# The last pair of batches attends one batch after the other, and four steps of its first batch run on GpSimd

## The chip, the cores and the metric

The kernel runs on one core of one Trainium2 chip. The metric is device time in microseconds (us), from the program's start to its end. TensorE (PE in the profile; PEld is its weight load) multiplies, VectorE (DVE), ScalarE (ACT) and GpSimd (POOL) do elementwise work, and SyncE (SP) issues the transfers.

## The reference

A layer with two parts over x of 32 batches, 512 tokens, 256 features, all float32:

```python
x = x + attention(layernorm(x))    # logits = phi phi^T * decay / temp, causal, softmax, times V
x = x + slots(layernorm(x))        # below

h = gelu(concat(x, slot_mean) @ w1.T + b1)
top = top_k((h @ w2.T + b2) / (abs(tau) + 0.1), 8)
alpha = softmax over the 8 chosen of 64 slots, zero elsewhere    # (T, 64)
gi = (alpha.T @ x) / (alpha.sum(0) + 1e-8)                        # (64, 256)
S_new = GRU(gi, slots)
out = (alpha @ (S_new @ wv.T + bv)) @ wo.T + bo
```

phi has 64 features per token; it comes from a tanh charge, random Fourier features and a combining matrix.

## The kernel before, in words

The batches go in 16 pairs. Pair k holds batches 2k (d = 0) and 2k + 1 (d = 1); the last pair is k = 15, batches 30 and 31. Every engine has its own queue, in which the steps of several pairs are mixed in an order written out by hand: a loop for the steady part and a long list for the end. An engine runs its queue strictly in that order; a step waits on semaphores that others raise, and all behind it wait with it.

The steps of a pair, each a function called with (k, ...), and the engine of each:

- **Attention.** phi (PE) and qk_full (DVE) give QK, in which batch d of the pair lies in partitions 64d to 64d + 63. The 512 query rows of a batch are four blocks of 128 rows; block i sees (i + 1) x 128 columns. logits(k, j) (PE) does blocks 0 and 1 (j = 0), block 2 (j = 1) or block 3 (j = 2), in each for the two batches alternately, into two banks of a ring L. Then for each of the eight row blocks n of a pair: row_max (DVE), expo (ACT), e_t (PE, i + 1 transpositions), probs_t (ACT, makes Eh), probs_low (DVE, makes El), values (PE, 3(i + 1) matmuls, the last i + 1 of which read El), attended (DVE, adds to X), lm_stats (DVE). Before, block n of every pair is row block n // 2 of batch n % 2, so the two batches go alternately.
- **Second norm.** lm_scale (six small operations of lm_variance_ops, and a power, on POOL), lm_norm (four operations, POOL) make xm; xm_t (PE), xm_copy (ACT), xm_low (DVE).
- **Routing.** hidden (PE), gelu (ACT), route (PE), rt_out (ACT), rt_t (PE), top (DVE, two max and two replace each, for half a batch), shift (DVE), shift8 (POOL), route_exp (ACT), weight_sum and chosen (DVE), alpha (POOL).
- **Slots.** gather (PE), gathered (DVE), gi_t (PE), gi_copy (ACT), gx_rz and gx_n (PE), gates, candidate (DVE), tanh (ACT), slot_change (POOL), new_slots (DVE), slot_v (PE), slot_values (DVE), al_t (PE), al_copy (ACT).
- **Output.** out_mm (PE), finish (DVE), store (SP).

In the last pair, before, the second norm (but for its power), shift8 and alpha of both batches run on DVE (end_scale, end_norm, end_shift, end_alpha, a for batch 30 and b for batch 31), and routing is done batch by batch (end_route, end_rt_t; gather(15) does batch 30's four matmuls, then batch 31's). warm(12) is twelve matmuls whose result nobody reads. residual adds X through an identity matmul, full array, two of 512 columns.

Lines that the rows name: L321 transpositions, L415 logits, L443 values, L497 end_route, L506 end_rt_t, L531 gather, L546 gates of the GRU, L656 residual; L1103 probs_low, L1119 attended, L1130 lm_stats, L1158 max of top; L246 and L258 the first and the last operation of lm_variance_ops, L1572 the power, L268 lm_norm, L287 alpha.

## Time and profile before

| | us |
|---|---|
| median of 3 runs | 689.96 (689.7 to 691.14) |
| the profiled execution | 689.95 |
| its span, first to last instruction | 688.1 |
| TensorE busy | 672.6 (98%) |
| VectorE busy | 605.0 (88%) |
| ScalarE busy | 514.3 (75%) |
| GpSimd busy | 386.9 (56%) |

Busy time is the time in which an engine had an instruction under way; matmuls overlap, and their ends are modelled, so their starts are the surer reading. The granted clock of TensorE is at its full level over the span but for the first slice and the last microseconds.

### The profile page before, as it was taken

The page shows a single profiled execution, that of the slowest core. Times are in us where ns is not written, and L with a number is a line of the kernel's source. Part 1 is how long each engine was busy: PE and PEld are TensorE (multiplying, and loading weights), DVE is VectorE, ACT ScalarE, POOL GpSimd, SP SyncE. Part 2 cuts the span into 40 slices and gives each one's busy share as a digit, 9 for nine tenths or more (in the row PEclk, how much of TensorE's full clock was granted, in tenths as well). Part 3 has the DMA queues.
Part 4 walks back from the last instruction along what each step waited for, and adds up shares of the span by engine and source line. Part 5 has one row for each costly group of instructions (what it writes and reads, how often), then busy time and mean ns, then how long its engine had stood idle before and what let it go on. Part 6 is the DMA issues. An engine that isn't in the chain of part 4 may idle for free.

```text
span 688.1 us, 15845 instructions
## 1 busy us (share of the span) xinstructions
PE 672.6 (98%) x4626; PEld 541.6 (79%) x4626; DVE 605.0 (88%) x2001; ACT 514.3 (75%) x1478; POOL 386.9 (56%) x818
## 2 busy tenths in 40 slices
PE   8999999999899999999999999999999999999996
PEld 5867878787697887879798787979878787978774
DVE  6688998797989898998989899898989989899984
ACT  4979889777596896959698695968879596875461
POOL 3727867362665747376565737556583756655200
PEclk9999999999999999999999999999999999999999
DMA  8343020204233050323215042421504242121004
GB/s 237 109 153 93 1 63 1 63 2 137 49 103 81 20 158 11 122 63 118 67 38 148 2 125 61 123 63 57 130 1 134 53 123 62 63 62 63 1 32 152
DMA packets 49115, 54.11 MB, mean 79 GB/s; under 512 B 6212, under 2 KB 40582, under 8 KB 49030
## 3 DMA queue, kind: packets, MB, share of 16 engines
q1 hardware_dynamic: 48260, 52.57, 27.7%
q8 instruction: 38, 0.62, 0.4%
q10 hardware_dynamic: 770, 0.53, 0.3%
q14 instruction: 47, 0.39, 0.2%
HBM read 20.58 MB, written 16.78 MB: 54 GB/s over the span
## 4 chain that ended last, share of the span: by engine, by line
PE 87%; SPq 3%; DVE 3%; ACT 2%; issue 2%; POOL 2%; DMA 1%; DVEq 0%; ACTq 0%; POOLq 0%
PE ps L321 17%; PE ps L349 16%; PE ps L443 15%; PE ps L476 6%; PE ps L546 6%; PE ps L415 6%; PE ps L531 4%; PE ps L641 4%; PE ps L488 2%; SPq L1717 2%; PE ps L392 2%; PE ps L617 2%; PE ps L398 2%; PE ps L395 2%; PE ps L308 1%
## 5 line engine op out<-in xcount | busy, mean ns | idle before, releaser
L241 POOL TENSOR_TENSOR Z<-Z,QB 128x512 f32<-128x512 f32 x60 | 77.4, 1290 | 80.6 <-ACT Z L834 78.8
L779 ACT ACTIVATE xn<-X,rs 128x255 f32<-128x255 f32 x128 | 66.4, 599 | 72.0 <-POOL rs L1563 72.0
L349 PE MATMUL ps<-W1h,xh 128*128 128x354 f32 x256 | 88.6, 346 | 0.0
L443 PE MATMUL ps<-Vh,Eh 128*128 128x256 f32 x320 | 88.6, 304 | 0.0
L349 PE MATMUL ps<-W1h,xl 128*128 128x354 f32 x256 | 83.2, 325 | 0.6 <-DVE xl L1039 0.5
L349 PE MATMUL ps<-W1l,xh 128*128 128x354 f32 x256 | 83.0, 324 | 0.0
L443 PE MATMUL ps<-Vl,Eh 128*128 128x256 f32 x320 | 80.9, 280 | 0.0
L845 ACT ACTIVATE E<-ps,nmax 128x128 f32<-128x128 f32 (+3 forms) x128 | 67.9, 536 | 9.7 <-DVE nmax L1095 9.5
L1103 DVE TENSOR_TENSOR El<-ps,Eh 128x128 fp32r<-128x128 f32 (+3 forms) x128 | 61.7, 483 | 13.2 <-ACT Eh L855 11.7
L1046 DVE TENSOR_TENSOR Vl<-ps,Vh 128x256 fp32r<-128x256 f32 x128 | 53.5, 419 | 21.7 <-ACT Vh L804 19.3
L268 POOL TENSOR_SCALAR xm<-X,rs 128x256 f32<-128x256 f32 x120 | 68.0, 581 | 2.2 <-POOL rs L1572 1.0
L855 ACT ACTIVATE Eh<-ps 128x128 fp32r<-128x128 f32 (+3 forms) x128 | 55.6, 445 | 11.8 <-PE ps L321 10.2
L443 PEld LDWEIGHTS ps<-Vh,Eh 128*128 128x128 f32 x320 | 60.3, 188 | 4.8 <-DVE X L1119 2.4
L1095 DVE CUSTOM_DVE_ANT_0 ps<-ps,causal 128x128 f32<-128x128 f32 (+3 forms) x128 | 60.9, 499 | 2.8 <-PE ps L415 2.8
L1119 DVE SCALAR_TENSOR_TENSOR X<-ps,rinv,X 128x256 f32<-128x256 f32 x128 | 59.5, 474 | 1.6 <-PE ps L443 1.2
L443 PEld LDWEIGHTS ps<-Vl,Eh 128*128 128x128 f32 x320 | 60.4, 189 | 0.2
L443 PE MATMUL ps<-Vh,El 128*128 128x256 f32 x320 | 58.7, 281 | 1.3 <-DVE El L1103 1.3
L321 PE MATMUL ps<-ident,E 128*128 128x128 f32 x320 | 55.3, 277 | 0.7 <-DVE El L1103 0.4
L1130 DVE BATCH_NORM_STATS2 stats<-X 128x6 f32<-128x256 f32 x128 | 51.8, 416 | 0.1
L804 ACT ACTIVATE Vh<-ps 128x256 fp32r<-128x256 f32 x128 | 51.7, 404 | 0.0
L349 PEld LDWEIGHTS ps<-W1h,xh 128*128 128x128 f32 x256 | 48.4, 189 | 2.9 <-issue 1.1
L321 PEld LDWEIGHTS ps<-ident,E 128*128 128x128 f32 x320 | 36.7, 140 | 17.5 <-issue 10.5
(245 smaller groups left out, 1961.9 us busy)
## 6 DMA issues: line engine op xcount, KB each, us to landing
X<-in_x SPq DMA_DIRECT2D x32, 512.0 KB, 4.4
xmT<-Z SPq DMA_DIRECT2D x120, 128.0 KB, 2.3
out_x<-X SPq DMA_DIRECT2D x30, 512.0 KB, 3.7
out_x<-X SPq DMA_DIRECT2D x4, 256.0 KB, 2.5
X<-in_gru_whhT SPq DMA_DIRECT2D x1, 768.0 KB
wih<-in_gru_wihT SPq DMA_DIRECT2D x1, 768.0 KB, 6.1
X<-in_W_v ACTq DMA_DIRECT2D x1, 256.0 KB, 4.5
X<-in_W_outT ACTq DMA_DIRECT2D x1, 256.0 KB
```

The lines of the kernel that those rows point to most:

```text
L241: e.tensor_tensor(Z[:, i + 1, :], Z[:, i, :], QB[:, :], ALU.mult).then_inc(s["zm"], 1)
L268: ins = e.tensor_scalar(xm[:, b % 3, t, 0:D], X[:, b % NX, t, :], rs2[:, d, 2, t:t + 1], rs2[:, d, 1, t:t + 1], ALU.add, ALU.mult)
L321: ins = e.transpose(p[0:m, j * 128:j * 128 + 128], block_in, ident[:, :])
L349: ins = e.matmul(p[:, 0:FEATS], x[:, d, c, t * 128:t * 128 + 128], w[:, c, :], start=j == 0, stop=j == 5)
L443: ins = e.matmul(p[:, 0:D], w[:, r % 2, j * 128:j * 128 + 128], v[:, (2 * k + d) % 4, j, :], start=z == 0, stop=z == len(parts) - 1)
L779: ins = e.activation(xn[:, d, t, 0:D - 1], X[:, b % NX, t, 0:D - 1], ACT.Identity, bias=rs[:, d, 2, t:t + 1], scale=rs[:, d, 1, t:t + 1])
L845: e.activation(E[:, r % 3, 0:w], at["lg", r], ACT.Exp, bias=nmax[:, r % 8:r % 8 + 1], scale=-1.0, accum_out=rsum[:, r % 8:r % 8 + 1]).then ...
L855: e.activation(Eh[:, r % 2, 0:w], at["E", r][:, 0:w], ACT.Copy).then_inc(s["eh"], 1)
L1046: e.tensor_tensor(Vl[:, b % 4, t, :], at["vs", b, t][:, 0:D], Vh[:, b % 4, t, :].bitcast(FP), ALU.subtract).then_inc(s["vl"], 1)
L1095: e.tensor_tensor_reduce(at["lg", r], at["lg", r], causal[:, N - w:N], 1.0, 3e38, ALU.add, ALU.min, nmax[:, r % 8:r % 8 + 1]).then_inc(s[" ...
L1103: e.tensor_tensor(El[:, r % 2, 0:w], at["E", r][:, 0:w], Eh[:, r % 2, 0:w].bitcast(FP), ALU.subtract).then_inc(s["ET"], 1)
L1119: e.scalar_tensor_tensor(X[:, b % NX, i, :], at["av", r][:, 0:D], rinv[:, r % 8:r % 8 + 1], X[:, b % NX, i, :], ALU.mult, ALU.add).then_in ...
```

## The change

Three things are done together.

1. In the last pair, block n is row block n % 4 of batch n // 4, so batch 30's four blocks come first and batch 31's four after them. A new end_logits(d, j) makes the logits of one batch; the waits are renumbered (place, width, shared, rows_done).
2. Batch 30's variance chain, normalization, shift8 and alpha go back from VectorE to GpSimd. Batch 31's stay on VectorE.
3. The order of the end, from the last pair's first norm on, is new on TensorE, ScalarE, VectorE and GpSimd. Some instances: rt_t(14) comes behind values(15, 4) and e_t(15, 6), where it came behind values(15, 3) and e_t(15, 4); top(14) comes behind lm_stats(15, 3), attended(15, 4) and probs_low(15, 5) on VectorE; finish(13, 1, 0) comes behind the last alpha. From gather(15) on TensorE's order is as before. SyncE's order is not changed.

```diff
--- before.py
+++ after.py
@@ -242,7 +242,7 @@
 
         def lm_variance_ops(e, k, d):
             b = 2 * k + d
-            e.wait_ge(s["lm_s"], 8 * k + 7 + d)
+            e.wait_ge(s["lm_s"], rows_done(k, d))
...
@@ -293,6 +293,20 @@
+        def place(k, n):
+            return divmod(n, 4) if k == NP - 1 else (n % 2, n // 2)
+
+        def width(k, n):
+            return place(k, n)[1] * 128 + 128
+
+        def shared(k, n):
+            if k == NP - 1:
+                return 1 if n % 4 == 0 else 0
+            return 2 if n < 2 else 0
+
+        def rows_done(k, d):
+            return 8 * k + 4 * d + 4 if k == NP - 1 else 8 * k + d + 7
...
@@ -415,6 +429,19 @@
+            def end_logits(d, j):
+                k = NP - 1
+                p, before = L.take(s["E"], 8 * k + 4 * d + j + 2)
+                if d == j == 0:
+                    e.wait_ge(s["qk"], 2 * k + 2)
+                if before:
+                    e.wait_ge(*before)
+                for i, c in ((0, 0), (1, 128)) if j == 0 else ((j + 1, 0),):
+                    rows, w = slice(i * 128, i * 128 + 128), i * 128 + 128
+                    at["lg", 8 * k + 4 * d + i] = p[:, c:c + w]
+                    e.matmul(p[:, c:c + w], QK[own(d), 0, rows], QK[own(d), 1, 0:w], start=True,
+                             stop=True, skip_group_check=True).then_inc(s["lg_mm"], 1)
...
-                transposes(p, [E[:, r % 3, j * 128:j * 128 + 128] for j in range(n // 2 + 1)]).then_inc(s["ET_t"], 1)
+                transposes(p, [E[:, r % 3, j * 128:j * 128 + 128] for j in range(place(k, n)[1] + 1)]).then_inc(s["ET_t"], 1)
...
-                i, d = divmod(n, 2)
+                d, i = place(k, n)
...
-                if n == 0:
-                    e.wait_ge(s["vl"], 8 * k + 8)
+                if i == 0 and (n == 0 or k == NP - 1):
+                    e.wait_ge(s["vl"], 8 * k + (4 * d + 4 if k == NP - 1 else 8))
...
-            e_t(14, 6); values(14, 5); values(14, 6); e_t(14, 7); phi(15); gather(13); logits(15, 0)
-            out_mm(12, 0); gi_t(13); values(14, 7); e_t(15, 0); xm_t(14, 0, 0); e_t(15, 1); gx_rz(13)
-            values(15, 0); e_t(15, 2); xm_t(14, 0, 1); gx_n(13); out_mm(12, 1); logits(15, 1); e_t(15, 3)
-            values(15, 1); xm_t(14, 1, 0); hidden(14, 0); xm_t(14, 1, 1); values(15, 2); hidden(14, 1)
-            e_t(15, 4); logits(15, 2); route(14); values(15, 3); rt_t(14); e_t(15, 5); slot_v(13)
-            values(15, 4); e_t(15, 6); values(15, 5); e_t(15, 7); al_t(13); values(15, 6); values(15, 7)
-            gather(14); out_mm(13, 0); gi_t(14); gx_rz(14); xm_t(15, 0, 0); xm_t(15, 0, 1); xm_t(15, 1, 0)
-            gx_n(14); xm_t(15, 1, 1); hidden(15, 0); hidden(15, 1); end_route(0); al_t(14); end_rt_t(0)
-            end_route(1); out_mm(13, 1); end_rt_t(1); slot_v(14); warm(12); gather(15); out_mm(14, 0)
...
+            e_t(14, 6); slot_v(12); values(14, 6); phi(15); gather(13); end_logits(0, 0); end_logits(0, 1)
+            e_t(14, 7); gi_t(13); out_mm(12, 0); end_logits(0, 2); e_t(15, 0); values(14, 7); e_t(15, 1)
+            gx_rz(13); end_logits(1, 0); end_logits(1, 1); xm_t(14, 0, 0); values(15, 0); xm_t(14, 0, 1)
+            values(15, 1); e_t(15, 2); gx_n(13); e_t(15, 3); e_t(15, 4); hidden(14, 0); end_logits(1, 2)
+            out_mm(12, 1); xm_t(14, 1, 0); xm_t(14, 1, 1); values(15, 2); hidden(14, 1); values(15, 3)
+            route(14); e_t(15, 5); values(15, 4); e_t(15, 6); rt_t(14); values(15, 5); slot_v(13); al_t(13)
+            values(15, 6); e_t(15, 7); xm_t(15, 0, 0); values(15, 7); gather(14); out_mm(13, 0); gi_t(14)
+            xm_t(15, 0, 1); gx_rz(14); xm_t(15, 1, 0); xm_t(15, 1, 1); hidden(15, 0); gx_n(14); hidden(15, 1)
+            end_route(0); al_t(14); end_route(1); end_rt_t(0); slot_v(14); end_rt_t(1); out_mm(13, 1)
+            warm(12); gather(15); out_mm(14, 0); gi_t(15); al_t(15); end_gx_r(); end_gx_nz(); out_mm(14, 1)
...
-                w = (n // 2 + 1) * 128
-                e.wait_ge(s["nmax"], r + 3 if n < 2 else r + 1)
+                w = width(k, n)
+                e.wait_ge(s["nmax"], r + 1 + shared(k, n))
...
+            gelu(14, 1); probs_t(15, 4); rt_out(14); probs_t(15, 5); probs_t(15, 6); expo(15, 7)
+            route_exp(14, 0); probs_t(15, 7); route_exp(14, 1); al_copy(13); xm_copy(15, 0, 0); gi_copy(14)
...
-                b, i = 2 * k + n % 2, n // 2
+                d, i = place(k, n)
+                b = 2 * k + d
                 e.wait_ge(s["av_mm"], r + 1)
-                e.wait_ge(s["rinv"], 4 * k + i + 1)
+                e.wait_ge(s["rinv"], 4 * k + n // 2 + 1)
...
-            def end_scale_a_setup():
-                e.wait_ge(s["lm_n"], B - 2)
-                lm_variance_ops(e, NP - 1, 0)
-
             def end_scale_b_setup():
+                e.wait_ge(s["lm_v"], B - 1)
                 lm_variance_ops(e, NP - 1, 1)
 
-            def end_norm_a_setup():
-                e.wait_ge(s["lm_n"], B - 2)
-                lm_norm_ops(e, NP - 1, 0)
-
             def end_norm_b_setup():
+                e.wait_ge(s["lm_n"], B - 1)
                 lm_norm_ops(e, NP - 1, 1)
 
-            def end_shift_a_setup():
-                e.wait_ge(s["dm8"], B - 2)
-                shift8_ops(e, NP - 1, 0)
-
             def end_shift_b_setup():
+                e.wait_ge(s["dm8"], B - 1)
                 shift8_ops(e, NP - 1, 1)
 
-            def end_alpha_a_setup():
-                e.wait_ge(s["am"], B - 2)
-                alpha_ops(e, NP - 1, 0)
-
             def end_alpha_b_setup():
+                e.wait_ge(s["am"], B - 1)
                 alpha_ops(e, NP - 1, 1)
...
-            attended(15, 3); top(14, 0, 0); top(14, 0, 1); top(14, 1, 0); shift(14, 0); top(14, 1, 1)
-            attended(15, 4); probs_low(15, 5); shift(14, 1); slot_values(13); probs_low(15, 6)
-            lm_stats(15, 3); attended(15, 5); chosen(14, 0); inverse(15, 3); weight_sum(14, 0)
-            probs_low(15, 7); weight_sum(14, 1); chosen(14, 1); attended(15, 6); lm_stats(15, 4)
-            lm_stats(15, 5); lm_stats(15, 6); attended(15, 7); end_scale_a_setup(); gathered(14)
-            lm_stats(15, 7); end_scale_b_setup(); finish(13, 0, 0); end_norm_a_setup(); end_norm_b_setup()
...
+            attended(15, 3); lm_stats(15, 3); attended(15, 4); probs_low(15, 5); top(14, 0, 0); top(14, 0, 1)
+            probs_low(15, 6); top(14, 1, 0); weight_sum(14, 0); shift(14, 0); top(14, 1, 1); shift(14, 1)
+            chosen(14, 0); attended(15, 5); weight_sum(14, 1); probs_low(15, 7); chosen(14, 1)
+            slot_values(13); lm_stats(15, 4); inverse(15, 3); lm_stats(15, 5); attended(15, 6)
+            attended(15, 7); lm_stats(15, 6); lm_stats(15, 7); gathered(14); end_scale_b_setup()
+            xm_low(15, 0, 0); finish(13, 0, 0); end_norm_b_setup(); xm_low(15, 0, 1); gates(14)
+            finish(13, 0, 1); xm_low(15, 1, 0); xm_low(15, 1, 1); candidate(14); new_slots(14); top(15, 0, 0)
+            top(15, 0, 1); top(15, 1, 0); shift(15, 0); top(15, 1, 1); weight_sum(15, 0); chosen(15, 0)
+            shift(15, 1); end_shift_b_setup(); slot_values(14); weight_sum(15, 1); chosen(15, 1)
+            end_alpha_b_setup(); finish(13, 1, 0); finish(13, 1, 1); gathered(15); finish(14, 0, 0)
...
@@ -1566,14 +1580,14 @@
-                if k < NP - 1:
+                if k < NP - 1 or d == 0:
...
             @live
             def lm_norm(k, d):
-                if k == NP - 1:
+                if k == NP - 1 and d:
...
-            rnorm(15); slot_change(12); phase(15); power(15, 0); power(15, 1); power(15, 2); shift8(13, 0)
+            slot_change(12); rnorm(15); phase(15); power(15, 0); power(15, 1); power(15, 2); shift8(13, 0)
             power(15, 3); shift8(13, 1); alpha(13, 0); alpha(13, 1); lm_scale(14, 0); lm_norm(14, 0)
-            lm_scale(14, 1); lm_norm(14, 1); slot_change(13); shift8(14, 0); shift8(14, 1); alpha(14, 0)
-            alpha(14, 1); lm_scale(15, 0); lm_scale(15, 1); slot_change(14)
+            lm_scale(14, 1); lm_norm(14, 1); slot_change(13); lm_scale(15, 0); shift8(14, 0); lm_norm(15, 0)
+            shift8(14, 1); alpha(14, 0); alpha(14, 1); lm_scale(15, 1); slot_change(14); shift8(15, 0)
+            alpha(15, 0)
```

## Rows read from the trace of the kernel before

**Rows 1.** The page: engines' busy time, then VectorE groups with count, busy us, mean ns.

```profile
PE 672.6 (98%) x4626; PEld 541.6 (79%) x4626; DVE 605.0 (88%) x2001; ACT 514.3 (75%) x1478; POOL 386.9 (56%) x818
...
L1103 DVE TENSOR_TENSOR El<-ps,Eh 128x128 fp32r<-128x128 f32 (+3 forms) x128 | 61.7, 483 | 13.2 <-ACT Eh L855 11.7
...
L1119 DVE SCALAR_TENSOR_TENSOR X<-ps,rinv,X 128x256 f32<-128x256 f32 x128 | 59.5, 474 | 1.6 <-PE ps L443 1.2
L1130 DVE BATCH_NORM_STATS2 stats<-X 128x6 f32<-128x256 f32 x128 | 51.8, 416 | 0.1
```

**Rows 2.** Busy time by stretch: length, each engine's busy us (instructions), clock, DMA.

```profile
639.71:649.28 9.57, 9.01 (x73) 8.19 (x73) 9.50 (x46) 4.85 (x13) 1.71 (x4) 1.00 0.01 2
643.13:669.08 25.95, 23.95 (x166) 18.69 (x165) 22.85 (x92) 12.54 (x24) 3.98 (x5) 1.00 0.07 22
```

**Rows 3.** The chain that ended last, from 616 on: start us, us, what.

```profile
619.32 1.74 PE ps L531 x16
...
621.06 0.86 PE ps L415 x8
...
630.04 0.65 PE ps L415 x4
...
636.09 1.06 PE ps L415 x4
...
644.31 0.87 PE ps L321 x8
645.18 2.81 PE ps L443 x24
647.99 2.29 PE ps L531 x16
...
660.59 1.05 PE ps L497 x2
...
665.17 0.24 PE ps L506 x4
...
669.15 2.81 PE ps L531 x16
...
677.98 1.91 PE ps L656 x4
```

**Rows 4.** TensorE in order of time: start us, us, in brackets idle before and releaser.

```profile
639.04 0.63 PE L321 MATMUL ps<-ident,hT 128*128 128x128 f32 x4
...
643.69 0.62 PE L443 MATMUL ps<-Vh,El 128*128 128x256 f32 x3 [0.56 <-DVE El L1103]
...
652.30 2.02 PE L546 MATMUL ps<-GI,wih 128*128 128x128 f32 x16 [0.56 <-ACT GI L903]
...
662.49 0.43 PE L506 MATMUL ps<-ident,hT 64*128 64x64 f32 x4 [0.28 <-ACT hT L886]
```

**Rows 5.** VectorE in order of time, from top(14) to the last alpha.

```profile
639.71 0.36 DVE L1158 MAX8 m<-ps 128x8 f32<-128x64 f32 x2
...
648.81 0.47 DVE L1119 SCALAR_TENSOR_TENSOR X<-ps,rinv,X 128x256 f32<-128x256 f32 x1
...
649.98 0.16 DVE L258 TENSOR_TENSOR rs<-rs 128x4 f32<-128x4 f32 x1
...
652.34 0.16 DVE L258 TENSOR_TENSOR rs<-rs 128x4 f32<-128x4 f32 x1
...
653.03 2.66 DVE L268 TENSOR_SCALAR xm<-X,rs 128x256 f32<-128x256 f32 x8
...
669.44 0.43 DVE L287 TENSOR_TENSOR AL<-lg,asum 128x256 f32<-128x256 f32 x1
```

**Rows 6.** GpSimd in order of time: the second norm of batch 28.

```profile
619.28 0.20 POOL L246 TENSOR_TENSOR mv<-stats 128x8 f32<-128x8 f32 x1 [0.23 <-DVE stats L1130]
...
621.01 1.04 POOL L1572 TENSOR_TENSOR rs<-rs,half 128x4 f32<-128x4 f32 x1
...
622.22 2.18 POOL L268 TENSOR_SCALAR xm<-X,rs 128x256 f32<-128x256 f32 x4 [0.17 <-POOL rs L1572]
```

More of the change, by code:

```diff
@@ L742, in _ @@
                 e_t(n, 7); values(n, 6); values(n, 7); phi(p); gather(f); logits(p, 0); out_mm(m, 0); gi_t(f)
-            xn_t(15, 0, 0); xn_t(15, 0, 1); gx_rz(12); proj(15, 0, 0); gx_n(12); e_t(14, 0); xn_t(15, 1, 0)
-            proj(15, 0, 1); xn_t(15, 1, 1); proj(15, 0, 2); proj(15, 0, 3); e_t(14, 1); logits(14, 1)
-            out_mm(11, 1); xm_t(13, 0, 0); proj(15, 1, 0); values(14, 0); xm_t(13, 0, 1); e_t(14, 2)
-            proj(15, 1, 1); proj(15, 1, 2); proj(15, 1, 3); values(14, 1); e_t(14, 3); xm_t(13, 1, 0)
@@ L747, in _ @@
-            xm_t(13, 1, 1); hidden(13, 0); q_t(15); hidden(13, 1); values(14, 2); e_t(14, 4); values(14, 3)
-            route(13); logits(14, 2); z_t(15); e_t(14, 5); rt_t(13); values(14, 4); al_t(12); slot_v(12)
-            e_t(14, 6); values(14, 5); values(14, 6); e_t(14, 7); phi(15); gather(13); logits(15, 0)
-            out_mm(12, 0); gi_t(13); values(14, 7); e_t(15, 0); xm_t(14, 0, 0); e_t(15, 1); gx_rz(13)
-            values(15, 0); e_t(15, 2); xm_t(14, 0, 1); gx_n(13); out_mm(12, 1); logits(15, 1); e_t(15, 3)
@@ L757, in _ @@
-            end_route(1); out_mm(13, 1); end_rt_t(1); slot_v(14); warm(12); gather(15); out_mm(14, 0)
-            gi_t(15); al_t(15); end_gx_r(); end_gx_nz(); out_mm(14, 1); residual(); slot_v(15); out_mm(15, 0)
-            out_mm(15, 1)
+            xn_t(15, 0, 0); xn_t(15, 0, 1); gx_rz(12); proj(15, 0, 0); proj(15, 0, 1); e_t(14, 0); gx_n(12)
+            xn_t(15, 1, 0); xn_t(15, 1, 1); proj(15, 0, 2); proj(15, 0, 3); logits(14, 1); out_mm(11, 1)
+            xm_t(13, 0, 0); proj(15, 1, 0); xm_t(13, 0, 1); values(14, 0); e_t(14, 1); proj(15, 1, 1)
@@ new lines, in _ @@
+            proj(15, 1, 2); values(14, 1); e_t(14, 2); e_t(14, 3); proj(15, 1, 3); xm_t(13, 1, 0)
+            xm_t(13, 1, 1); hidden(13, 0); e_t(14, 4); values(14, 2); hidden(13, 1); values(14, 3); q_t(15)
+            logits(14, 2); route(13); z_t(15); e_t(14, 5); rt_t(13); values(14, 4); values(14, 5); al_t(12)
+            e_t(14, 6); slot_v(12); values(14, 6); phi(15); gather(13); end_logits(0, 0); end_logits(0, 1)
+            e_t(14, 7); gi_t(13); out_mm(12, 0); end_logits(0, 2); e_t(15, 0); values(14, 7); e_t(15, 1)
@@ L1520, in _ @@
-            mirror(15); quarter_turn(15); attended(14, 3); lm_stats(14, 2); probs_low(14, 4); inverse(14, 2)
-            lm_stats(14, 3); row_max(14, 6); row_max(14, 7); top(13, 0, 0); top(13, 0, 1); attended(14, 4)
-            probs_low(14, 5); top(13, 1, 0); top(13, 1, 1); shift(13, 0); probs_low(14, 6); shift(13, 1)
-            slot_values(12); chosen(13, 0); attended(14, 5); inverse(14, 3); weight_sum(13, 0); chosen(13, 1)
-            lm_stats(14, 4); lm_stats(14, 5); weight_sum(13, 1); attended(14, 6); lm_stats(14, 6); qk_full(15)
@@ L1541, in _ @@
[L1541 to L1545 removed]
+            slot_values(11); ln_stats(15, 0, 0); weight_sum(12, 1); chosen(12, 1); ln_stats(15, 0, 1)
@@ new lines, in _ @@
+            attended(13, 6); lm_stats(13, 3); ln_stats(15, 1, 0); attended(13, 7); qk_full(14)
+            ln_stats(15, 1, 1); lm_stats(13, 4); gathered(12); row_max(14, 0); finish(11, 0, 0)
+            finish(11, 0, 1); row_max(14, 1); xn_low(15, 0, 0); xn_low(15, 0, 1); lm_stats(13, 5); gates(12)
+            row_max(14, 2); lm_stats(13, 6); row_max(14, 3); v_low(15, 0, 0); inverse(14, 0); probs_low(14, 0)
+            lm_stats(13, 7); v_low(15, 0, 1); candidate(12); inverse(14, 1); v_low(15, 0, 2); xn_low(15, 1, 0)
@@ new lines, in _ @@
+            lm_stats(14, 0); lm_stats(14, 1); row_max(14, 6); row_max(14, 7); lm_stats(14, 2)
+            probs_low(14, 5); top(13, 0, 0); attended(14, 4); lm_stats(14, 3); top(13, 0, 1); attended(14, 5)
+            shift(13, 0); top(13, 1, 0); probs_low(14, 6); top(13, 1, 1); chosen(13, 0); shift(13, 1)
+            lm_stats(14, 4); weight_sum(13, 0); chosen(13, 1); weight_sum(13, 1); inverse(14, 3)
+            slot_values(12); qk_full(15); attended(14, 6); gathered(13); row_max(15, 0); row_max(15, 1)
@@ L1609, in shift8 @@
             def shift8(k, d):
-                if k == NP - 1:
+                if k == NP - 1 and d:
                     return
@@ L1616, in alpha @@
             def alpha(k, d):
-                if k == NP - 1:
+                if k == NP - 1 and d:
                     return
```

79 lines of the change are left out of this document (33 added, 46 removed).

## The prediction

> **What bounds the kernel now.** I read the page first: TensorE is busy 98% of the span, VectorE 88% [rows 1]. So whatever the change does, it must act through the 2% in which TensorE stands, or through the length of TensorE's own work. Then the busy time by stretch: between 643.13 and 669.08 TensorE is busy 23.95 of 25.95 us, so 2.0 us of idle lie there, and between 639.71 and 649.28 it is VectorE that is full, 9.50 of 9.57 us [rows 2]. Then the chain of waits, for the pitch of each group of matmuls: the reader is to see there that some groups, of equal size, take different times [rows 3]. Then the order of time of TensorE, for its waits: 0.56 us for El of row block 5 of the last pair, 0.56 us for GI, 0.28 us for the routing logits [rows 4]. Last, VectorE's and GpSimd's own sequences, for the chain that the last batch goes through after its last values [rows 5, 6]. The tail from gather(15) on has the same order on TensorE before and after, so I carry it over unchanged; what I need is how much later or earlier gather(15) ends.
>
> **Pairs of logits are split: +1.8 us of TensorE.** logits(15, j) issues the two batches' matmuls alternately; they have a contraction of 64 and lie in the two halves of the partitions. Its three calls take 0.86, 0.65 and 1.06 us, 2.57 us for 2560 streamed columns [rows 3]. end_logits issues one batch at a time. What a 512-column matmul costs when its neighbour does not use the other half: end_route, one matmul, takes 1.05 us, as much as the 1.06 us of a pair of such; residual's two full-array ones take 1.91 us together [rows 3]. At residual's 0.96 us per 512 columns, 2560 columns take 4.8 us: +2.2 us; at end_route's, 5.25 us: +2.7. The lower end comes from gather: with the batches alternating it takes 1.74 us, in gather(15), where one batch follows the other, 2.81 us, a factor of 1.61 [rows 3], so +1.6 us. That factor is under 2 because the second batch's run begins while the first's is under way; in the new order this can happen once, where out_mm(12, 1) stands behind end_logits(1, 2), and I take 0.4 us off for it (one of its four matmuls). Value taken: 2.2 - 0.4 = +1.8 us, nearer to residual, since most neighbours of the new blocks are full-array matmuls. Nothing below zero: the same columns are streamed.
>
> The rows show two 64-deep matmuls of one size running in the time of one. The Trainium skill says the same of such matmuls in "TensorE: Matmul & The Clock Gate", section "Part 3: Packing small matmuls — row/col tiling", and adds that matmuls start and end strictly in program order. By that rule nothing would be gained at out_mm(12, 1), and the sum of this part would be +2.2; by gather(15)'s row it is +1.8.
>
> **The routing chain of pair 14 starts later.** rt_t(14) started at 639.04 [rows 4], and top(14) on VectorE at 639.71 [rows 5]. In the new order TensorE has done more of pair 15 when it comes to rt_t(14): values 0 to 4 with blocks of 1, 2, 3, 4, 1 (33 matmuls) where there were values 0 to 3 with 1, 1, 2, 2 (18): 15 x 0.117 (2.81 / 24) = 1.8 us; transposes of E 16 where there were 9: 7 x 0.109 (0.87 / 8) = 0.8 us [rows 3]; and the 1.8 us of the logits. Together 4.3 us (1.76 + 0.76 + 1.8); everything else that stood ahead of it still does. So top(14) begins at about 639.71 + 4.3 = 644.0. I assume that TensorE meets no new wait up to there; ScalarE and VectorE have more room in that part than later.
>
> **VectorE from there to attended(15, 7).** Before: 639.71 to 648.81 + 0.47 = 649.28, 9.57 us without a gap [rows 2, 5]. Now attended(15, 4), probs_low(15, 5) and lm_stats(15, 3) stand ahead of top(14), and lm_stats(15, 6) behind attended(15, 7): 0.47 + 0.48 + 0.42 + 0.42 = 1.8 us fewer [rows 1]. 644.0 + 7.8 = 651.8, which is 2.5 us later than before. This part is full on VectorE, so what it loses on TensorE the 0.56 us wait for El [rows 4] gives back only in part: TensorE stands at gather(14) for alpha(14, 1) as before, where gather took 2.29 us for work of 1.74 [rows 3].
>
> **The last batch's norm.** Before, the first of the two variance chains ended at 649.98 + 0.16 = 650.14 and the second at 652.50 [rows 5], 3.22 us behind attended(15, 7). The first chain, 0.86 us of it, is now on GpSimd, lm_stats(15, 6), 0.42 us, comes in: 2.8 us, so 654.6. GpSimd's power, about 1.1 us with its hand-over [rows 6], is hidden behind nothing as before. Then only four normalizations stand in VectorE's queue where there were eight in 2.66 us [rows 5]: 1.33 us. xm of batch 31 is ready at 654.6 + 1.2 + 1.33 = 657.1; it was ready at 653.03 + 2.66 = 655.69. So of 2.5 us that are late, 1.1 is given back here by the work that went to GpSimd, and +1.4 us stay. TensorE would be there earlier, at about 656, since it has only gather, out_mm, gi_t, one transposition and gx_rz in between, so it waits about 1 us.
>
> **From there to gather(15).** Before, 655.69 to 669.15, 13.46 us [rows 3, 5]. The set of TensorE's work is the same, xm_t(15, 1, 0) to warm, but end_rt_t(0) now stands behind end_route(1), so its wait of 0.28 us and the start-up behind it (its four 64-column transpositions take 0.24 us elsewhere) go [rows 3, 4]: -0.45, 13.0 us. gather(15) starts at 670.1, +0.95 us. VectorE is in step with that: alpha of batch 31 ended at 669.44 + 0.43 = 669.87, 4.7 us behind end_rt_t(1) at 665.17 [rows 3, 5]; end_rt_t(1) stays 4.0 us ahead of gather(15) (out_mm has taken slot_v's place behind it, both of one size), so alpha comes at 670.8, and gather(15)'s second half, which needs it, is as much later, +0.95. The two finish(13, 1) behind it fit under gather(15)'s 2.81 us, and the stores that they release have some 8 us until the next one: free.
>
> **The four steps on GpSimd** cost there 1.7 us (variance chain, 619.28 to 621.01), 1.0 (power) and 2.2 (normalization) [rows 6] besides shift8 and alpha, with nobody waiting for them as long as they are done before xm_t(15, 0, 0) and hidden(15, 0): values(15, 3) ends 1.95 us before rt_t(14) (route, as long as a pair of logits, 1.05, values(15, 4), three matmuls, 0.35, and five transpositions, 0.55), at 641.4; attended and lm_stats make it 642.3, so lm_norm(15, 0) ends near 642.3 + 1.8 + 1.1 + 2.2 = 647.4, or 647.7 with shift8(14, 0) ahead of it. In its queue behind it stand shift8(14, 1), alpha(14, 0) and alpha(14, 1). VectorE has m8 of (14, 1) at about 647.5: a tie, priced at nothing here and below as a rival.
>
> **Sum.** The profiled execution took 689.95 us, the median of the runs is 689.96, so both are one number here. 689.95 + 0.95 = 690.9 us, +0.14%. A measurement of this kernel can tell about 0.2% (1.4 us) from no change: 688.6 to 691.3 is no change.
>
> **Rivals.** *Faster: the waits go and the halves cost little.* All idle of 643.13 to 669.08, 2.0 us, and the 0.55 us of gather(14) are gained because VectorE has 10 instructions for statistics and 4 normalizations fewer, and the logits cost nothing: 689.95 - 2.55 = 687.4. With the logits at their lower end, +1.6, even this gives only 689.0. It decides if top(14) begins before about 641.5 at the new place. For it: VectorE is the engine without a gap there [rows 2]. Against it: rows 3 for the halves.
> *Neutral: the logits cost nothing, the rest as worked out:* everything above follows top(14) one for one, 690.9 - 1.8 = 689.1.
> *Slower: GpSimd's queue becomes the bound.* If batch 30's statistics come late, lm_norm(15, 0), 2.2 us in one piece, holds shift8(14, 1); ScalarE's exp waits for it, then weight_sum(14, 1) on VectorE, and behind that in the same queue probs_low(15, 7), for which values(15, 7) waits. There are some 0.7 us of work between (shift, chosen, attended) before it bites; from lm_norm ending at 648.4 on, each us costs a us. With 1 us late and the logits at their upper end: 690.9 + 1.0 + 0.9 = 692.8. For it: the order puts a 2.2 us step ahead of a 0.3 us one that others need. Likewise probs_t(15, 7) stands on ScalarE behind an exp that waits for shift(14, 0), which I priced at nothing.
>
> **Chances.** Forecast 0.45 (0.35 of it within 0.2%, 0.10 above, its upper part being only 0.4 us from the border); neutral 0.15; faster 0.20; slower by GpSimd 0.20. So faster 0.20, same 0.50, slower 0.30. The forecast's own range is 690.0 to 691.8; with the cases on both sides 688.2 to 692.9.
>
> **What the changed profile would show.** Groups of the new logits line whose 512-column matmul takes about 1 us alone; rt_t(14) near 643.4 and the first max of top(14) near 644.0; no wait of TensorE for El of block 5, but one of about 1 us before xm_t(15, 1, 0) released by VectorE's normalization; lm_norm of batch 30 on GpSimd between 645 and 648 and nobody waiting for what stands behind it; gather(15) starting near 670.1 and the same 16 us from its end to the end of the span. The prediction is wrong if the logits of one batch take as little as the pair did, if a wait arises earlier than 640 (the middle of the order is new too, and I walked only its end), or if weight_sum(14, 1) waits for GpSimd.

## The result, and the profile after

The changed kernel takes **692.38 us** (median of 8 runs, 691.47 to 694.4); the kernel before, on the same chip, 689.83 us (median of 8 runs, 689.01 to 691.14). The ratio is 1.0037, with an interval of 1.0024 to 1.005: slower by 2.55 us, or 0.37%. The forecast was 690.9 us with a range of 688.2 to 692.9. The time lies in the range, but above what the forecast's own case allowed (691.8), and on the slower side, to which 0.3 was given. It is in the range only because that takes in the slower rival's time, and that rival's mechanism did not occur; the hit is in part luck.

The profiled execution has a span of 690.9 us, where the one before had 688.1: +2.8 us. The page, first the engines' busy time, then VectorE's groups (count, busy us, mean ns, idle before them):

```profile
PE 675.4 (98%) x4626; PEld 542.6 (79%) x4626; DVE 602.9 (87%) x1989; ACT 514.9 (75%) x1478; POOL 389.1 (56%) x830
...
L1130 DVE TENSOR_TENSOR El<-ps,Eh 128x128 fp32r<-128x128 f32 (+3 forms) x128 | 61.8, 484 | 13.4 <-ACT Eh L882 12.1
...
L1147 DVE SCALAR_TENSOR_TENSOR X<-ps,rinv,X 128x256 f32<-128x256 f32 x128 | 59.6, 474 | 2.3 <-PE ps L470 1.9
```

Against [rows 1] twelve instructions have gone from VectorE to GpSimd (VectorE 2.1 us less, GpSimd 2.2 us more), and TensorE has as many instructions as before but is busy 2.8 us longer. The durations of single instructions are those of before. So the change of the span is there in TensorE's busy time, and the question is where.

TensorE in order of time, gather(12) (of batches 24 and 25) and gather(15) (of the last pair); first the kernel before, then the changed one (start, duration):

```profile
580.71 1.91 PE L531 MATMUL ps<-xm,AL 128*64 128x257 f32 x16
...
669.08 2.88 PE L531 MATMUL ps<-xm,AL 128*64 128x257 f32 x16
```

```profile
580.66 1.91 PE L558 MATMUL ps<-xm,AL 128*64 128x257 f32 x16
...
671.63 3.13 PE L558 MATMUL ps<-xm,AL 128*64 128x257 f32 x16
```

At gather(12) the two profiles agree within 0.05 us, and up to the end of gather(15) the changed one loses 2.80 us: (671.63 + 3.13) - (669.08 + 2.88). Nothing is lost or won after it: 16.1 us remain in both. The profiled executions of the experiments differ at gather(12) by up to 4 us (experiment 2, which changes the loop, apart), so below everything is counted from there.

The chain that ended last, in the changed kernel (start, us, what):

```profile
615.17 3.26 DMA xmT<-Z
...
618.48 1.08 PE ps L412 x4
619.56 1.74 PE ps L558 x16
621.30 1.49 PE ps L442 x6
...
623.60 1.06 PE ps L668 x8
624.66 0.85 PE ps L442 x2
...
629.18 1.49 PE ps L442 x6
...
635.93 0.42 PE ps L442
636.35 0.22 PE ps L668
636.56 0.22 PE ps L442
636.78 1.07 PE ps L668 x5
...
649.79 0.41 DVE X L1147
...
650.24 1.67 PE ps L470 x12
...
671.70 3.06 PE ps L558 x16
```

L442 is the new line of the logits. Its rows give 1.49 + 0.85 + 1.49 + 0.42 + 0.22 = 4.47 us where [rows 3] have 2.57 us. At the top of the fence the chain runs through a transfer: the last third of phi(15) waits for it, which it did not in the kernel before.

TensorE in order of time, its waits in brackets (rt_t(14) without one):

```profile
644.62 0.61 PE L335 MATMUL ps<-ident,hT 128*128 128x128 f32 x4
...
649.51 0.66 PE L335 MATMUL ps<-ident,xm 128*128 128x128 f32 x4 [0.78 <-DVE lg L1198]
...
658.74 1.06 PE L335 MATMUL ps<-ident,xm 128*128 128x128 f32 x8 [0.53 <-DVE xm L268]
```

All the waits of [rows 4], for El, GI and the routing logits, are gone. rt_t(14) starts 5.58 us later than before. The 0.78 us stand ahead of xm_t(15, 0, 0), which needs batch 30's normalization. The page names a subtraction on VectorE (L1198) as releaser, but the instruction reads xm, and xm's last write, on GpSimd, ended at 647.06 + 2.16 = 649.22 (below): that is very likely the wait. The prediction had nobody waiting for this step. The wait cost next to nothing all the same: in the chain above values(15, 7), which stands behind xm_t(15, 0, 0), starts at 650.24 and is put down to attended(15, 5) on VectorE (649.79 + 0.41).

Busy time from top(14) to the end of attended(15, 7) (length, then PE, PEld, VectorE, ScalarE, GpSimd):

```profile
645.28:653.24 7.96, 7.11 (x55) 6.16 (x55) 7.89 (x43) 4.63 (x11) 5.21 (x11) 1.00 0.01 2
```

This stretch answers to the first of [rows 2]: VectorE is full again (7.89 of 7.96 us), but in 7.96 us, not 9.57. VectorE itself, in order of time:

```profile
645.28 0.36 DVE L1186 MAX8 m<-ps 128x8 f32<-128x64 f32 x2
...
652.37 0.86 DVE L1147 SCALAR_TENSOR_TENSOR X<-ps,rinv,X 128x256 f32<-128x256 f32 x2
...
657.21 1.38 DVE L268 TENSOR_SCALAR xm<-X,rs 128x256 f32<-128x256 f32 x4
...
670.23 0.42 DVE L1198 TENSOR_TENSOR lg<-ps,m 128x256 f32<-128x256 f32 x1
670.56 0.55 DVE L277 TENSOR_TENSOR m8s<-m 128x32 f32<-128x32 f32 x1
...
672.33 0.42 DVE L287 TENSOR_TENSOR AL<-lg,asum 128x256 f32<-128x256 f32 x1 [0.19 <-DVE lg L1214]
```

attended(15, 7) ends at 653.23 (649.28 before), xm of batch 31 is ready at 657.21 + 1.38 = 658.59 (655.69 before), and alpha of batch 31 at 672.75 (669.87 before). So the loss is 5.6 us at top(14), 3.95 at attended(15, 7), 2.90 at xm, 2.55 at the start of gather(15) and 2.80 at its end. GpSimd, in the same stretch:

```profile
645.82 1.04 POOL L1586 TENSOR_TENSOR rs<-rs,half 128x4 f32<-128x4 f32 x1
646.83 0.24 POOL L277 TENSOR_TENSOR m8s<-m 128x32 f32<-128x32 f32 x1
647.06 2.16 POOL L268 TENSOR_SCALAR xm<-X,rs 128x256 f32<-128x256 f32 x4
649.19 0.24 POOL L277 TENSOR_TENSOR m8s<-m 128x32 f32<-128x32 f32 x1
```

shift8(14, 1), the fourth row, starts right behind the normalization of 2.16 us, and also right behind the last step of top(14, 1) on VectorE, which ended at 649.12: the tie on which the slower rival hung came out even, and VectorE did not stand ahead of weight_sum(14, 1).

### The profile page after: what moved, and what is told of

The parts are those of the page before. It is cut to its first block, busy times and chain, and to the rows that moved or that the text cites. A ratio compares the mean times of both kernels' runs of the same rounds, so it can differ in the third digit from the quotient of the medians.

```text
span 690.9 us, 15845 instructions
## 1 busy us (share of the span) xinstructions
PE 675.4 (98%) x4626; PEld 542.6 (79%) x4626; DVE 602.9 (87%) x1989; ACT 514.9 (75%) x1478; POOL 389.1 (56%) x830
## 4 chain that ended last, share of the span: by engine, by line
PE 85%; SPq 3%; DVE 3%; ACT 3%; POOL 2%; issue 2%; DMA 2%; DVEq 0%; POOLq 0%; ACTq 0%
PE ps L335 17%; PE ps L363 16%; PE ps L470 14%; PE ps L573 6%; PE ps L503 6%; PE ps L429 5%; PE ps L558 4%; PE ps L668 4%; SPq L1732 2%; PE ps L515 2%; PE ps L412 2%; PE ps L406 2%; PE ps L644 2%; PE ps L409 2%; POOL Z L241 1%
## 5 line engine op out<-in xcount | busy, mean ns | idle before, releaser
L268 POOL TENSOR_SCALAR xm<-X,rs 128x256 f32<-128x256 f32 x124 | 69.8, 576 | 2.2 <-POOL rs L1586 1.0
L1169 DVE TENSOR_TENSOR xmL<-ps,xmT 128x512 fp32r<-128x512 f32 x62 | 42.2, 686 | 9.9 <-ACT xmT L893 9.6
```

Source lines behind the costliest of these rows:

```text
L268: ins = e.tensor_scalar(xm[:, b % 3, t, 0:D], X[:, b % NX, t, :], rs2[:, d, 2, t:t + 1], rs2[:, d, 1, t:t + 1], ALU.add, ALU.mult)
```

## The experiments

The table first. Its time columns are medians (the ratio with its interval is against the kernel before, run beside each); the other columns are worked out from TensorE's order of time in each profile: the start of gather(13), (14), (15) behind the start of gather(12), how long gather(15) took, and where it ended.

| kernel | median us (runs) | ratio to before | g(13) | g(14) | g(15) | took | end | end against before |
|---|---|---|---|---|---|---|---|---|
| before | 689.83 (8) | | 38.44 | 67.21 | 88.37 | 2.88 | 91.25 | |
| changed | 692.38 (8) | 1.0037 (1.0024 to 1.005) | 38.73 | 71.18 | 90.97 | 3.13 | 94.10 | +2.85 |
| before, logits split | 693.72 (6) | 1.0054 (1.0036 to 1.0072) | 38.51 | 70.62 | 91.79 | 2.88 | 94.67 | +3.42 |
| changed, e_t first | 693.12 (6) | 1.005 (1.0033 to 1.0067) | 39.50 | 71.52 | 91.31 | 3.12 | 94.43 | +3.18 |
| changed, end_rt_t first | 693.23 (6) | 1.0045 (1.0031 to 1.006) | 38.26 | 70.82 | 90.92 | 3.12 | 94.04 | +2.79 |
| before, four steps on GpSimd | 690.91 (11) | 1.0017 (1.0008 to 1.0026) | 38.43 | 67.18 | 89.33 | 2.88 | 92.21 | +0.96 |
| changed, four steps on VectorE | 697.46 (4) | 1.0112 (1.0098 to 1.0125) | 38.25 | 75.88 | 95.36 | 3.16 | 98.52 | +7.27 |
| the same, better placed | 694.49 (5) | 1.0063 (1.0051 to 1.0076) | 38.42 | 72.65 | 92.47 | 3.16 | 95.63 | +4.38 |
| changed, shift8 first | 692.15 (6) | 1.0033 (1.0021 to 1.0045) | 38.27 | 70.80 | 90.61 | 2.88 | 93.49 | +2.24 |
| changed, logits twice | 696.66 (4) | 1.0101 (1.0085 to 1.0116) | 38.51 | 75.30 | 95.09 | 3.12 | 98.21 | +6.96 |
| before, end_route(1) first | 690.74 (11) | 1.0011 (1.0001 to 1.002) | 38.47 | 67.23 | 89.18 | 3.00 | 92.18 | +0.93 |

The last column and the medians agree within about half a microsecond, so this column can be used where a median is too coarse, though each row of it is one execution. For the experiments the kernel before had medians of 689.94, 689.65 and 689.9 us. The changed kernel's own row contains a wait of 0.4 to 0.5 us ahead of gather(13) that most of the other executions go without (experiment 4), so an experiment that goes without it looks up to that much better beside this row than it is; where it matters the count starts at gather(13).

**1. The split of the logits alone.**

```
-  phi(15); gather(13); logits(15, 0); out_mm(12, 0); gi_t(13); values(14, 7)
+  phi(15); gather(13); out_mm(12, 0); logits_of_one(15, 0, 0); gi_t(13); logits_of_one(15, 0, 1); values(14, 7)
...
-  logits(15, 1); e_t(15, 3)
+  logits_of_one(15, 1, 0); e_t(15, 3); logits_of_one(15, 1, 1)
-  e_t(15, 4); logits(15, 2); route(14)
+  logits_of_one(15, 2, 0); e_t(15, 4); logits_of_one(15, 2, 1); route(14)
```

> The kernel before, with one thing of the change: in the last pair, the two batches' logits are issued apart, with a full-array step between them; the order of attention, the engines of all steps and the rest of the order stay. Theory (half of the change's loss is TensorE's own work, because a 64-deep matmul without a partner in the other half takes as long as a pair): the changed kernel's logits took 4.69 us where the pairs took 2.57, so TensorE gets 2.1 us more; at most 0.56 us of it vanish in the wait for El at 643.69, so 1.5 to 2.1 us slower than before, and the 512-column blocks take about 1 us each in the chain. Rival (the logits lie under VectorE's work, and the loss comes from the order): within 0.3 us of before.

Measured: +3.8 us by the medians, +3.42 us by the profile. The chain of this kernel, at the new line (L430) and at two neighbours (L656 out_mm, L458 values):

```profile
624.11 1.06 PE ps L656 x8
625.17 0.65 PE ps L430 x4
...
626.18 0.85 PE ps L430 x4
627.03 1.60 PE ps L458 x12
...
634.20 0.64 PE ps L430 x2
...
635.20 0.84 PE ps L430 x2
...
640.95 1.05 PE ps L430 x2
...
642.48 1.05 PE ps L430 x2
```

The six rows of L430 make 5.08 us against 2.57 us for the same matmuls in pairs: +2.51 us. Most of the remaining 0.9 us stands in the rows of neighbours, each against the same group in the chain of before: out_mm(12, 0) 1.06 for 0.86, values(14, 7) 1.60 for 1.41, values(15, 1) 0.56 for 0.36, e_t(15, 4) 0.48 for 0.33: 0.74 us for four groups that now begin anew. The result is above what was expected. It is also more than the whole change costs, though it splits more finely than the change does (5.08 against 4.47 us for the logits): the rest of the change does give something back.

**2. The same split in ten pairs of the loop.** Three edits of the same kind in the loop's own order, where the calls also change places with neighbours.

> The kernel before, with the same separation of the two batches' logits in the ten pairs of the steady loop, where TensorE is busy 39.99 of 40 us, the last two pairs left as they are. Theory: 10 x 2.1 = 21 us slower, 19 to 23. If adjacent halves did not overlap in truth, or the time is hidden: under 3 us.

Measured: 719.3 us (4 runs, 718.57 to 720.52), ratio 1.0425 (1.0409 to 1.0442): +29.4 us, 2.9 us for each pair. The page:

```profile
PE 701.2 (98%) x4626; PEld 551.1 (77%) x4626; DVE 606.3 (84%) x2001; ACT 516.6 (72%) x1478; POOL 386.5 (54%) x818
```

With the same number of instructions TensorE is busy 28.6 us longer, and the time is 29.4 us longer, above the 19 to 23 expected. In the chain one pair's logits (from 312.65 us on) take 5.01 us, where a pair of the kernel before (from 303.72 on) has 2.76: 2.25 us of the 2.9; the rest lies beside them, as in experiment 1. This amplified run leaves no doubt about sign and size: two 64-deep matmuls in the two halves of the partitions, issued in turn, cost about what one costs (1.06 us for a pair of 512 columns), and with a full-array group between them each costs that (1.05 us).

**3. The logits' price doubled in place.**

```
                     e.matmul(p[:, c:c + w], QK[own(d), 0, rows], QK[own(d), 1, 0:w], start=True,
-                             stop=True, skip_group_check=True).then_inc(s["lg_mm"], 1)
+                             stop=True, skip_group_check=True)
+                    e.matmul(p[:, c:c + w], QK[own(d), 0, rows], QK[own(d), 1, 0:w], start=True,
+                             stop=True, skip_group_check=True).then_inc(s["lg_mm"], 1)
```

> The changed kernel with each matmul of the last pair's logits issued twice (the second overwrites the first with the same numbers), so their price is doubled in place. My theory: what the logits cost on TensorE ahead of rt_t(14) is carried to the end one for one, because the routing chain of pair 14 and all of VectorE's full part start from rt_t(14). The profile shows 4.7 us for them, so rt_t(14), gather(15) and the median come 4.7 us later (4.2 to 5.2): 697.1, +1.04% against the kernel before. Rival (VectorE or ScalarE has its own limit in that part and TensorE has slack): 2 to 3.5 us, 694.5 to 696.

Measured: gather(14) 4.12 us later than in the changed kernel, gather(15) 4.12 us later, the median 4.3 us, at the lower edge of what was expected. The chain, first logits as they were (L442) and second (L444):

```profile
625.34 0.85 PE ps L442 x2
626.19 0.86 PE ps L444 x2
```

A 512-column matmul behind its like takes 0.86 us, so the 2560 columns are 4.3 us without start-ups. Counted from gather(13), which leaves out the changed kernel's longer wait ahead of it, gather(14) and gather(15) come 4.34 us later: all of it arrives at the end. TensorE's work ahead of rt_t(14) is carried through to the end one for one, in spite of a VectorE that is full behind rt_t(14): it is full because its work starts from there.

**4. phi(15)'s wait for its transfer taken away.**

```
-  values(14, 6); phi(15); gather(13); end_logits(0, 0); end_logits(0, 1); e_t(14, 7)
+  values(14, 6); e_t(14, 7); phi(15); gather(13); end_logits(0, 0); end_logits(0, 1)
...
-  probs_t(14, 6); route_exp(13, 0); route_exp(13, 1); expo(14, 7)
+  expo(14, 7); probs_t(14, 6); route_exp(13, 0); route_exp(13, 1)
```

> The changed kernel, with e_t(14, 7) ahead of phi(15) again and expo(14, 7) early enough for it; nothing else. Theory: the changed order took 0.44 us of TensorE's work away from ahead of phi(15), whose last third waits for transfers that arrive when they did before, and about 0.6 to 0.8 us of the loss arose there; the wait of 0.26 us shrinks or goes and gather(13) starts at the same time with 0.44 us less behind it: 0.4 to 0.7 us faster than the changed kernel. Rival (what is late on GpSimd and VectorE from 645 on sets the end whatever happens at 618): no difference to the changed kernel within 0.2 us, gather(15) at 671.7 again.

Measured: no gain (693.12 us; gather(15) 91.31 us behind gather(12) where it was 90.97). The wait went from the transfer to e_t(14, 7) itself:

```profile
616.21 0.66 PE L335 MATMUL ps<-ident,E 128*128 128x128 f32 x4 [0.62 <-DVE lg L1198]
```

The expectation failed, but the column g(13) tells what the changed kernel's wait is worth. Five experiments (3, 5, 7 and the two of 9) have the changed kernel's order up to gather(13). In three of them the last third of phi(15) follows the one ahead of it after 0.86 us, as in the kernel before, and gather(13) starts 38.25 to 38.27 us behind gather(12). In experiment 3 it follows after 1.08 us and in the second of 9 after 0.92, and gather(13) starts at 38.51 and 38.42; in the changed kernel's own profile after 1.28 us, and at 38.73. So the wait cost 0.4 to 0.5 us in that one execution, up to 0.2 in others and nothing in most. The profiled execution took 692.74 us, 0.36 above the kernel's median, which fits.

**5. end_rt_t(0) ahead of end_route(1) again.**

```
-  end_route(0); al_t(14); end_route(1); end_rt_t(0); slot_v(14)
+  end_route(0); al_t(14); end_rt_t(0); end_route(1); slot_v(14)
```

> The changed kernel, with end_rt_t(0) ahead of end_route(1) on TensorE as in the kernel before. Theory: in the changed kernel VectorE stands 1.18 us before top(15, 0) because that transposition waits in TensorE's queue behind end_route(1), and from there to the last alpha VectorE is the chain: 0.6 to 0.9 us faster than the changed kernel, last alpha at about 672.0 for 672.75. Rival (TensorE's own list with warm sets gather(15)): no gain, or 0.2 us slower for the wait that comes back on TensorE.

Measured: a miss, and the rival's outcome. From gather(14) to gather(15) it takes 20.10 us where the changed kernel takes 19.79: 0.3 us longer. VectorE's top(15, 0) starts earlier, but it then stands 1.03 us waiting for end_rt_t(1) ahead of top(15, 1), and the last alpha comes no sooner. So it was not this order that cost time.

**6. The other way round, in the kernel before.**

```
-  end_route(0); al_t(14); end_rt_t(0); end_route(1)
+  end_route(0); al_t(14); end_route(1); end_rt_t(0)
```

> The kernel before with one term of the third part alone: end_rt_t(0) behind end_route(1) on TensorE, so that its wait of 0.28 us and the start-up behind it go. My theory: gather(15) starts 0.3 to 0.45 us earlier, counted from gather(12), 689.3 to 689.5; in the profile only, since a median tells no such difference. Rival (VectorE's chain from top(15, 0) on, which now starts about 0.8 us later, sets alpha of batch 31): gather(15) starts earlier but takes longer than 2.88 us and its end does not move or comes later, 689.7 to 690.2.

Measured: 0.93 us slower by the profile, 0.8 us by the medians, the rival's direction and more of it. TensorE in order of time:

```profile
664.02 1.04 PE L497 MATMUL ps<-hT,w 128*64 128x512 f32 x2 [0.85 <-ACT hT L877]
...
670.83 3.00 PE L531 MATMUL ps<-xm,AL 128*64 128x257 f32 x16 [0.54 <-DVE AL L287]
```

end_route(1) now waits 0.85 us for ScalarE's hT, time that end_rt_t(0) had filled, and gather(15) waits 0.54 us for alpha. The 0.28 us of wait that it was to save were the cheaper place to stand.

**7. shift8 of batch 31 ahead of shift(15, 1).**

```
-  shift(15, 1); end_shift_b_setup(); slot_values(14); weight_sum(15, 1)
+  end_shift_b_setup(); shift(15, 1); slot_values(14); weight_sum(15, 1)
```

> The changed kernel with one swap on VectorE: shift8 of batch 31 ahead of shift(15, 1), as in the order before, not behind it. In the changed kernel's profile the exponential of m8s starts 0.04 us behind that shift8's end and weight_sum(15, 1) waits for it, 0.75 us from shift's end where it was 0.25 us before; gather's last matmuls wait for the alpha behind it. My theory: alpha of batch 31 comes 0.4 to 0.5 us earlier, and gather(15) takes 2.8 us where it took 3.06: -0.25 to -0.3 us, so 692.1, within the noise of a median but to be seen in the profile. Rival (TensorE's own list sets the end, alpha has slack): gather(15) takes 3.06 us as before and nothing moves, 692.4.

Measured, TensorE and then VectorE in order of time:

```profile
670.28 2.88 PE L558 MATMUL ps<-xm,AL 128*64 128x257 f32 x16
```

```profile
668.88 0.18 DVE L277 TENSOR_TENSOR m8s<-m 128x32 f32<-128x32 f32 x1
668.99 0.42 DVE L1198 TENSOR_TENSOR lg<-ps,m 128x256 f32<-128x256 f32 x1
...
670.54 0.42 DVE L287 TENSOR_TENSOR AL<-lg,asum 128x256 f32<-128x256 f32 x1 [0.19 <-issue]
```

gather(15) takes 2.88 us again, not 3.13, as expected. Alpha ends 0.68 us behind gather(15)'s start where it ended 1.12 us behind it. Small as it is, it shows that in the changed kernel VectorE's chain, not TensorE's list, set the end of gather(15). Part of the gain is that shift8 takes 0.18 us at its new place and took 0.55 at the old one (last section). The medians (692.15 against 692.38) can't tell the 0.25 us.

**8. The four steps on GpSimd alone, in the kernel before.** Batch 30's variance chain, normalization, shift8 and alpha go to GpSimd, all other orders stay.

```
-  alpha(14, 1); lm_scale(15, 0); lm_scale(15, 1); slot_change(14)
+  alpha(14, 1); lm_scale(15, 0); lm_norm(15, 0); lm_scale(15, 1); slot_change(14); shift8(15, 0); alpha(15, 0)
```

> The second part alone: in the kernel before, batch 30's variance chain, normalization, shift8 and alpha go to GpSimd; all other orders, the pairs of logits too, stay. My theory: this part gives something back only because the change finishes batch 30 early. In the old order its last statistics come at 649.2, so on GpSimd the norm of batch 30 ends only about 5 us later (chain 1.7, power 1.0, norm 2.2: 654.1), with power of batch 31 behind it, and xm of batch 31 is ready no earlier than before (+0.9 at most, less 0.45 for what leaves VectorE): between no change and +0.5 us against the kernel before, so 690 to 690.5. Rival: VectorE is what bounds the end, and 2.7 us less of its work is worth something in any order: 688.5 to 689.

Measured: +1.2 us by the medians, +0.96 by the profile, so slower than expected but of the expected sign. First GpSimd in order of time, then TensorE with its wait:

```profile
653.35 2.23 POOL L268 TENSOR_SCALAR xm<-X,rs 128x256 f32<-128x256 f32 x4 [0.17 <-POOL rs L1576]
655.54 1.00 POOL L1576 TENSOR_TENSOR rs<-rs,half 128x4 f32<-128x4 f32 x1
```

```profile
658.27 0.63 PE L321 MATMUL ps<-ident,xm 128*128 128x128 f32 x4 [1.48 <-DVE xm L268]
```

The normalization ends at 655.6 only, and batch 31's power stands behind it. In the old order GpSimd is too slow for these steps; they pay only because the changed order has batch 30's normalization done 4.8 us earlier (counted from gather(12), 649.22 - 580.66 against 655.58 - 582.18).

**9. The four steps back on VectorE in the changed kernel.**

```
-  attended(15, 3); lm_stats(15, 3); attended(15, 4)
+  attended(15, 3); lm_stats(15, 3); end_scale_a_setup(); attended(15, 4)
-  chosen(14, 1); slot_values(13)
+  chosen(14, 1); end_norm_a_setup(); slot_values(13)
```

and shift8 and alpha of batch 30 behind top(15, 0, 1) and chosen(15, 0).

> The changed kernel with the second part undone: the four steps of batch 30 are on VectorE again (variance chain behind lm_stats(15, 3), normalization behind chosen(14, 1), shift8 behind top(15, 0, 1), alpha behind chosen(15, 0)); TensorE's and ScalarE's orders stay as changed. My theory: VectorE is full from top(14) to attended(15, 7), so the normalization's 1.33 us and part of the chain's 0.86 there, and some 0.4 us for shift8 and alpha at the end, come back: +1.3 to +2.3 us against the changed kernel, 693.7 to 694.7. Rival (GpSimd's steps hold others up: the power and the norm between shift8(14, 0) and shift8(14, 1), and alpha of batch 30 shares time with VectorE at the end): the changed kernel gains by undoing it, 691.5 to 692.4.

Measured: +5.1 us against the changed kernel, far more than expected, because of the place of the normalization. TensorE in order of time:

```profile
653.29 1.09 PE L335 MATMUL ps<-ident,xm 128*128 128x128 f32 x4 [4.42 <-DVE xm L268]
```

A second version has end_norm_a_setup() behind top(14, 0, 1):

> The second part undone again in the changed kernel, better placed: the run before it left TensorE 4.4 us waiting ahead of xm_t(15, 0, 0), since batch 30's normalization stood behind chosen(14, 1) on VectorE. Now it stands behind top(14, 0, 1). My theory: VectorE is full from top(14) to attended(15, 7), so 1.33 us of normalization and the variance chain's part come back there, and some 0.4 us at the end: gather(15) 1.3 to 2.3 us later than in the changed kernel, 693.7 to 694.7. Rival (VectorE has slack once the work is placed well; only the place cost the time): within 0.5 us of the changed kernel, 692 to 693.

Measured: +2.1 us by the medians, +1.53 us by the profile against the changed kernel, 1.84 us counted from gather(13). That is what the second part of the change is worth once the others have been made, against this placing on VectorE. gather(15) takes 3.16 us here, but with two more steps on VectorE, so this does not tell what GpSimd's alpha has to do with the 3.13 us of the changed kernel.

## Why the prediction came out as it did

**What bounds the kernel: right.** The 2.8 us are in TensorE's busy time, and doubling a part of it (experiment 3) moves the end one for one.

**The pairs of logits: mechanism right, term too small.** I took +1.8 us, as 2.2 minus 0.4 for overlap with out_mm(12, 1). The logits' own rows give +1.90 (4.47 - 2.57), but out_mm beside them changed too. In the kernel before, out_mm(12, 0) and (12, 1) were, in the chain:

```profile
621.92 0.86 PE ps L641 x8
...
628.97 1.06 PE ps L641 x8
```

together 1.92 us; now they are 1.06 + 0.22 + 1.07 = 2.35. Logits and out_mm together went from 4.49 to 6.82 us: +2.33 us, 0.5 more than predicted. I had looked for overlap that is won at the new seams, and not for the cheap start that out_mm(12, 0) loses, for it stood behind a pair of logits. My yardsticks were of another shape, too: gather and end_route are 128 deep and 64 wide, the logits 64 deep and 128 wide. Fully separated (experiment 1) the logits cost 1.98 times the pairs, not gather's 1.61. At the seam of end_logits(1, 2) and out_mm(12, 1) the two take 0.42 + 0.22 + 0.22 + 1.07 = 1.93 us; the same two sizes in the other order, out_mm(12, 0) and end_logits(0, 2), take 1.06 + 0.85 = 1.91. So the seam is worth one start-up, about 0.2 us, whichever comes first, not the 0.4 I took off.
The Trainium skill's "Part 3: Packing small matmuls — row/col tiling" in "TensorE: Matmul & The Clock Gate", by which matmuls start and end in program order, gave +2.2 for this part. The trace does not agree with it on the order: a row of out_mm (636.35) stands between two rows of the logits (635.93, 636.56) that are ahead of it in the program. But the seam without such an exchange costs the same (1.91 against 1.93 us), and as an estimate of what logits and out_mm together cost, the rule's 2.2 was nearer to the 2.33 than my 1.8.

**"Together 4.3 us (1.76 + 0.76 + 1.8)": the step that failed.** rt_t(14) was predicted 4.3 us later and came 5.58 us later, so this sum was 1.3 us too small; the sentence behind it, "I assume that TensorE meets no new wait up to there", failed too. Of the 1.3 us, 0.5 are the term above. 0.4 to 0.5 are phi(15)'s wait for its transfer, in the profiled execution: e_t(14, 7) had stood ahead of phi(15), and I had walked only the end of the order, as the prediction says. The rest can be narrowed down by the place of e_t(14, 7), four transpositions or 0.44 us. With them gone from ahead of gather(13) it should start at 38.44 - 0.44 = 38.0 us behind gather(12); without any wait at phi(15) it starts at 38.25 to 38.27, so 0.25 us are lost in the new order between the two gathers, which no single row shows. Behind gather(13), up to rt_t(14), it takes 25.23 us where it took 19.89. The chain's rows give 2.33 us of that to logits and out_mm, 1.59 to the 15 matmuls of values (1.76 predicted), and 1.58 to eleven more transpositions, which at my 0.109 each are 1.20 (0.76 predicted and the 0.44 of e_t(14, 7)), so 0.4 us are their start-ups (these rows add up to 5.50 us, 0.16 more than lies between the starts). A new wait is thus the smaller part of the miss; the larger is that groups beside each other cost more in the new sequence than the same groups did in the old.

**VectorE's full part: right.** 7.95 us from top(14) to the end of attended(15, 7) where 7.8 were predicted and 9.57 were before. So it gave back the 1.6 us, and the loss there was 3.95 us in place of 2.5, all from the later start.

**The last batch's norm: right.** Predicted 1.1 us given back, measured 3.95 - 2.90 = 1.05. Experiments 8 and 9 show both sides of it: the GpSimd part costs 1 us in the old order and is worth 1.5 to 2.1 us in the new one. GpSimd's normalization of batch 30 ended at 649.22, not near 647.7, and TensorE waited 0.78 us for it, which the prediction did not have; it cost next to nothing, as shown above. TensorE waits 0.53 us ahead of xm_t(15, 1, 0), predicted about 1.

**From xm to gather(15): right, with luck in the reason.** Predicted 13.0 us, measured 671.70 - 658.59 = 13.11, before 13.46. In the new order the exchange of end_rt_t(0) and end_route(1) does save 0.3 us (experiment 5). But the reason was given from the rows of the old order, and there the same exchange costs 0.9 us (experiment 6). Which way it goes depends on whether gelu's output hT on ScalarE is done when end_route(1) comes.

**VectorE "in step" at the end: too small.** The last alpha was to come 4.7 us behind end_rt_t(1); it came 672.75 - 667.51 = 5.2 us behind. With shift8 of batch 31 behind shift(15, 1), the exponential that weight_sum(15, 1) needs starts later, and gather(15) took 3.06 us in the chain, not 2.81. Experiment 7 undoes this.

**The sum.** 3.95 - 1.05 - 0.35 + 0.25 = 2.80 us, where the prediction had 2.5 - 1.1 - 0.45 = 0.95. Of the difference of 1.85 us, 1.45 lie ahead of attended(15, 7) (1.3 of it on TensorE), 0.25 in gather(15), and 0.15 in the two terms between.

**The rivals.** The faster one needed top(14) before 641.5; it came at 645.28. The neutral one needed free logits. The slower one, GpSimd's queue, was nearest in time (692.8) but not in mechanism: its tie held. The kernel is slower because TensorE's part grew more than I took.

## What to carry to other kernels

When an order keeps apart two half-deep matmuls that ran as a pair, price it as twice the columns, and price the neighbours' start-ups too: here that was 0.15 to 0.2 us for each group that now begins anew. Count also the work that the order moves across a common milestone, and ask whether the milestone moved with it. Work on the engine that bounds the kernel comes out one for one at the end, even if another engine is full in the stretch behind it; and moving work to a slower engine paid here only because its input had become early enough, so the two parts of such a change can't be judged one by one. Before you let "no new wait" stand in a sum, walk the whole of the new order and ask of each wait-free group what stood ahead of it and covered it.
